# First edge stage of a graph-network kernel: both halves of a group's sums moved around the first filter layer, one group later

## The chip, the core and the metric

The kernel runs on one core of one Trainium2 chip. The metric is the device time in microseconds (us) of one execution. Three timed runs of the kernel before gave 2712.55 us as their median, with 2710.3 and 2718.26 us as the ends.

## What is computed

The reference is two layers of a graph network over 3125 nodes with 256 features and 50000 edges; each layer is a graph step and then a feed-forward step. The change touches only the first graph step, which is a continuous-filter convolution. Cut to what matters:

```python
W   = ssp(e_ji_basis @ fw1.T + fb1) @ fw2.T + fb2      # filter, one row per edge
W   = W * C[:, None]                                   # C from the edge's weight
h   = x @ w1.T                                         # node table
msg = h[src] * W                                       # gather, multiply
agg = jax.ops.segment_sum(msg, dst, num_segments=n)    # sum by target node
```

`ssp(x)` is `softplus(x) - log(2)`. The edges come sorted by target node.

## The kernel before, in words

The program is a row of stages with a barrier between them: preparation, the node table (`source_features`), the first edge stage (`edges_first`), the node update (`nodes_first`), a mixture of experts, the attention layer with an edge stage of its own (`attention_edges`), and the last feed-forward step. Each engine has its instructions written out by hand, in order, and engines meet only through semaphores. What matters here is `edges_first`.

The edges are cut into tiles of 256, and the 25 windows of 128 target nodes into the same list, so that there are 220 items of one tile and one window each. A **group** is two items, that is four chunks of 128 edges; there are 110 groups. For a group n the work is:

- SyncE loads the edge attributes `ea` (L533), four buffers, loaded seven groups ahead.
- ScalarE copies the group's source indices into `idx` (L319, `source_index`), and GpSimd gathers the node rows with four indirect transfers (L312, `gather`) into `rows`, four buffers of it, three groups ahead.
- TensorE computes the first filter layer into PSUM, two matmuls of 512 columns: `z(n)` (L581), two buffers.
- ScalarE takes Exp (L626) and Ln (L628) of it into `soft`, VectorE takes the result `hid` (L661), ScalarE rounds that to its high part `hidh` (L636), VectorE forms the low part `hidl` (L644). Each has two buffers.
- TensorE computes the second filter layer, 28 matmuls of 256 columns: `w(n)` (L592 to L596), in one PSUM buffer `wp`.
- VectorE builds the four scaled one-hot tiles `hot` (L652) and multiplies `wp` with the gathered rows into `msg` (L670), two buffers each.
- TensorE adds each item into the running window: `add(n, 0)` and `add(n, 1)`, two matmuls each (L567, `add_item`). There are two PSUM banks for windows, used in turn. After each item ScalarE copies the bank's sum to SBUF (L614) and clears the *other* bank (L615, `keep`), and the next item's matmuls wait for that (semaphore `s_acc`).

So between two items there is a round trip: TensorE ends an item, ScalarE copies and clears, TensorE may begin the next item. That holds for every pair of items, within a group and across groups.

The order on each engine is given by a function `step`, called once per group; `at(k)` is the group k ahead of the step's own n. Before the change TensorE's step n was

```python
add(n, 0);  z(n + 4);  w(n + 1);  add(n, 1)
```

and ScalarE's was

```python
keep(n, 0);  exp, ln(n + 4);  idx(n + 4);  hidh(n + 3);  keep(n, 1)
```

and VectorE's is `hot(n + 1)`, `hid(n + 3)`, `hidl(n + 2)`, `msg(n + 1)`. `rounds` (L293) writes the first steps out, puts the middle into a hardware loop of `UNROLL` steps a round, and writes the last steps out. `UNROLL` is 4. A buffer's number is the group's number modulo the number of buffers (`slot`, `slot4`), and `turn4` counts how often a buffer was used. The attention stage has a class of its own (`Edges`) and gathers of its own, so it does not use what is changed here.

Of the kernel before, what the change touches and what calls it, by code (L numbers as in the profile page):

```python
# [16 lines left out]
F32 = mybir.dt.float32  # L17
F32R = mybir.dt.float32r
I32 = mybir.dt.int32
# [234 lines left out]
class Group:  # L254


    COUNT, UNROLL = NIG, 4

    def __init__(self, it, q):
        self.n = it * 4 + q  # L260
        self.slot, self.turn = q % 2, it * 2 + q // 2
        self.slot4, self.turn4 = q % 4, it + q // 4
# [44 lines left out]
def gather(c, pool, g, idx, rows, table, s_rows, s_idx, s_used):  # L307


    need(pool, c.sem("poolgate"), (s_idx, g.n + 1), (s_used, g.n - 3))  # L310
    for j in range(IG):
        c.nc.gpsimd.indirect_dma_start(out=rows[:, g.slot4, j, :], out_offset=None, in_=table,  # L312
                                       in_offset=bass.IndirectOffsetOnAxis(ap=idx[:, g.slot4, j:j + 1], axis=0)).then_inc(s_rows[g.slot4], 16)


def source_index(c, act, g, idx, s_rows, s_idx):

    need(act, c.sem("actgate"), (s_rows[g.slot4], g.turn4 * 64))
    c.nc.scalar.copy(idx[:, g.slot4, :], c.src_i[:, bass.ds(g.n * IG, IG)]).then_inc(s_idx, 1)  # L319
# [169 lines left out]
def edges_first(c, A):  # L489
# [7 lines left out]
    with ExitStack() as s:  # L497
# [20 lines left out]
        s_rows = [c.sem(f"e1_rows{p}") for p in range(4)]  # L518
# [3 lines left out]
        with nc.Block() as block:  # L522
# [20 lines left out]
            @block.gpsimd  # L543
            def _(pool):
                nc.gpsimd.memset(zero[:, :], 0.0).then_inc(s_zero, 1)
                pool.wait_ge(s_zero, 1)
                nc.gpsimd.memset(ea[GA:P, :, :], 1.0 / GA).then_inc(s_cst, 1)
                pool.wait_ge(s_cst, 1)

                def step(at):  # L550
                    g = at(3)
                    if real(g):
                        gather(c, pool, g, idx, rows, c.h_dram, s_rows, s_idx, s_msg)
                rounds(pool, step, 3, 0)

            @block.tensor
            def _(pe):
# [4 lines left out]
                def add_item(g, j, wins):  # L562

                    need(pe, None, (s_msg, g.n + 1), (s_acc, g.n * JG + j), own=True)
                    for half in range(CT):
                        t = j * CT + half
                        last = mm(bank(wins[j]), hot[:, g.slot, t, :], msg[:, g.slot, t, :], start=False, stop=False, skip_group_check=True)  # L567
                    last.then_inc(s_agg, 1)

                def step(at):  # L570
                    a = at(0)
# [4 lines left out]
                    if real(g):  # L576
# [5 lines left out]
                        last.then_inc(s_z, 1)  # L582
                    g = at(1)
                    if real(g):

                        need(pe, None, (s_hl, g.n + 1), (s_msg, g.n), own=True)
                        for j in range(IG):
# [3 lines left out]
                            for k in range(KC):  # L591
                                mm(w, hidl[:, g.slot, cols[k]], w2h[:, k, :], start=(k == 0), stop=False)  # L592
                                mm(w, hidh[:, g.slot, cols[k]], w2l[:, k, :], start=False, stop=False)  # L593
                            mm(w, share[:, :], b2hl[:, :], start=False, stop=False)
                            for k in range(KC):
                                last = mm(w, hidh[:, g.slot, cols[k]], w2h[:, k, :], start=False, stop=(k == KC - 1))  # L596
# [44 lines left out]
            @block.vector  # L641
            def _(dve):
# [3 lines left out]
                def one_hot(g):  # L646
                    if real(g):

                        need(dve, s_dg, (s_agg, (g.n - 1) * JG))
                        for j in range(IG):  # L650
                            i = g.n * IG + j
                            v.scalar_tensor_tensor(hot[:, g.slot, j, :], c.iota_n[:, :], c.dst_rel[:, bass.ds(i, 1)],  # L652
                                                   c.coef[:, bass.ds(i, 1)].broadcast_to([P, P]), ALU.is_equal, ALU.mult)

                def step(at):
# [7 lines left out]
                    if real(h):  # L663

                        need(dve, s_dg, (s_hh, h.n + 1))
                        low(hidl[:, h.slot, :], hid[:, h.slot, :], hidh[:, h.slot, :]).then_inc(s_hl, 1)
                    if real(g):

                        need(dve, s_dg, (s_w, g.n + 1), (s_rows[g.slot4], (g.turn4 + 1) * 64))
                        v.tensor_tensor(msg[:, g.slot, :, :], wp[:, :].rearrange("p (a d) -> p a d", a=IG), rows[:, g.slot4, :, :], ALU.mult).then_inc(s_msg, 1)  # L670
# [1256 lines left out]
```

## Time and profile before

| | us |
|---|---|
| median of three timed runs | 2712.55 |
| lowest and highest of them | 2710.3, 2718.26 |
| the profiled execution's own time | 2724.59 |
| its span in the trace | 2722.8 |

| stage | from | to, in us of the span |
|---|---|---|
| first edge stage, its first steps | 81 | 124 |
| its even part | 124 | 1007 |
| its last steps, with no first layer left | 1007 | 1035 |

All times below are microseconds from the start of the span. The profiled execution took 12.0 us more than the median of the timed runs, and 1.8 us more than its span. A row of the timeline gives start, duration, engine, line, operation, what is written and what is read, and how many instructions were merged; in brackets the idle time of the engine before it and what ended it. An "x4" of a 32-bit matmul line is two matmuls, since the trace holds two records for each. The end of a matmul is modelled, so that records of matmuls that follow each other overlap.

### The profile page before, as it was taken

How to read it: one execution, taken by the hardware profiler on the slowest of the kernel's cores; microseconds unless marked ns; L12 is line 12 of the kernel's file. 1: busy time of each engine (PE TensorE's matmuls, PEld its weight loads, DVE VectorE, ACT ScalarE, POOL GpSimd, SP SyncE). 2: the span in 40 equal slices, each digit the busy share in tenths (PEclk: the TensorE clock that was granted, in tenths of full speed). 3: DMA queues.
4: the chain of work that ended last, by engine and by line, in shares of the span. 5: the costliest groups of instructions: out<-in, count | busy, mean ns of one | idle time of the engine just before them, and what ended most of it. 6: DMA issues, size and time to landing. Idle time of an engine off the chain costs nothing. (4 is left out here: it accounts for less than half of the span.)

```text
span 2722.8 us, 44123 instructions
## 1 busy us (share of the span) xinstructions
PE 2098.0 (77%) x11608; PEld 1731.4 (64%) x11609; DVE 1692.7 (62%) x3111; ACT 880.7 (32%) x1743; POOL 1098.4 (40%) x1037
## 2 busy tenths in 40 slices
PE   5588888888888888699995757877777777753498
PEld 4366666666666667699995645655555555532498
DVE  4355555555555554656556538887878788858565
ACT  2355555555555544344441101111111111100143
POOL 0355555555555544500001046555665656311200
PEclk8799999999999998799998968888989889867699
DMA  3222222222222220200000355554545545310100
GB/s 99 91 80 77 77 80 78 77 77 79 78 78 79 77 62 1 78 1 0 0 1 16 123 158 145 144 155 139 162 140 147 150 143 150 97 49 3 33 20 29
DMA packets 104782, 222.93 MB, mean 82 GB/s; under 512 B 19802, under 2 KB 58726, under 8 KB 104550
## 3 DMA queue, kind: packets, MB, share of 16 engines
q0 software_dynamic: 56320, 173.07, 21.9%
q1 hardware_dynamic: 48358, 48.68, 5.5%
q8 instruction: 40, 0.66, 0.1%
q14 instruction: 64, 0.52, 0.1%
HBM read 205.29 MB, written 16.38 MB: 81 GB/s over the span
## 5 line engine op out<-in xcount | busy, mean ns | idle before, releaser
L312 POOL DMA_INDIRECT e_rows<-h_table,e_idx x440 | 511.6, 1163 | 419.9 <-ACT e_idx L319 308.5
L1404 POOL DMA_INDIRECT a_rows<-kv_table,a_idx x440 | 466.2, 1060 | 389.6 <-issue 150.9
L670 DVE TENSOR_TENSOR e_msg<-e_w,e_rows 128x1024 f32<-128x1024 f32 x110 | 134.7, 1225 | 438.8 <-PE e_w L596 423.0
L1471 PE MATMUL a_q<-q,a_spread 128*128 x880 | 273.8, 465 | 126.4 <-ACT a_spread L1447 91.4
L567 PE MATMUL e_agg<-e_msg,e_hot 128*128 128x256 f32 x880 | 238.6, 394 | 169.8 <-ACT e_agg L615 153.0
L1471 PEld LDWEIGHTS a_q<-q,a_spread 128*128 128x128 f32 x880 | 191.2, 228 | 174.6 <-issue 145.6
L567 PEld LDWEIGHTS e_agg<-e_msg,e_hot 128*128 128x128 f32 x880 | 150.9, 190 | 225.3 <-issue 213.6
L592 PE MATMUL e_w<-w2h,e_hidl 128*128 128x256 f32 x880 | 271.2, 331 | 0.0
L1480 PE MATMUL a_agg<-a_rows,x 128*128 128x264 f32 x880 | 242.7, 424 | 18.7 <-DVE a_rows L1537 18.4
L1447 ACT COPY a_spread<-a_hotT 128x512 f32<-128x512 f32 x110 | 64.4, 585 | 522.7 <-PE a_hotT L1495 325.0
L593 PE MATMUL e_w<-w2l,e_hidh 128*128 128x256 f32 x880 | 227.8, 281 | 0.0
L1480 PEld LDWEIGHTS a_agg<-a_rows,x 128*128 128x128 f32 x880 | 188.1, 215 | 60.7 <-DVE a_rows L1537 16.3
L581 PE MATMUL e_z<-e_ea,w 128*128 128x512 f32 x440 | 210.3, 601 | 11.0 <-DMA e_ea<-in_eaT 8.7
L593 PEld LDWEIGHTS e_w<-w2l,e_hidh 128*128 128x128 f32 x880 | 166.7, 189 | 25.9 <-issue 25.9
L592 PEld LDWEIGHTS e_w<-w2h,e_hidl 128*128 128x128 f32 x880 | 166.1, 189 | 25.9 <-issue 25.6
L596 PE MATMUL e_w<-w2h,e_hidh 128*128 128x256 f32 x880 | 176.0, 281 | 0.0
L636 ACT CAST e_hidh<-e_hid 128x1024 fp32r<-128x1024 f32 x110 | 115.0, 1046 | 125.7 <-issue 74.5
L614 ACT COPY sums<-e_agg x220 | 81.9, 372 | 224.6 <-PE e_agg L567 212.7
L1550 DVE TENSOR_TENSOR a_rows<-a_q,a_rows 128x1024 f32<-128x1024 f32 x110 | 133.7, 1216 | 32.4 <-remote 18.6
L1531 DVE TENSOR_TENSOR sums<-sums,a_agg 128x264 f32 x220 | 93.5, 425 | 91.4 <-issue 47.4
L661 DVE SCALAR_TENSOR_TENSOR e_hid<-e_soft,e_z 128x1024 f32<-128x1024 f32 x110 | 133.4, 1213 | 20.8 <-ACT e_soft L628 20.8
L626 ACT ACTIVATE e_soft<-e_z 128x1024 f32<-128x1024 f32 x110 | 112.9, 1026 | 92.7 <-PE e_z L581 46.9
(338 smaller groups left out, 4705.3 us busy)
## 6 DMA issues: line engine op xcount, KB each, us to landing
e_ea<-in_eaT SPq DMA_DIRECT2D x220, 64.0 KB
e_rows<-h_table,e_idx POOLq DMA_INDIRECT x440
a_rows<-kv_table,a_idx POOLq DMA_INDIRECT x440
kv_table<-q_kv SPq DMA_DIRECT2D x25, 256.0 KB, 2.0
m_stage<-in_m_w SPq DMA_DIRECT2D x16, 256.0 KB, 2.7
x<-in_x SPq DMA_DIRECT2D x1, 3200.0 KB, 12.6
h_table<-n_h SPq DMA_DIRECT2D x5, 640.0 KB
x_table<-x SPq DMA_DIRECT2D x1, 3200.0 KB, 13.9
```

The costliest lines, as they stand in the source:

```text
L312: c.nc.gpsimd.indirect_dma_start(out=rows[:, g.slot4, j, :], out_offset=None, in_=table, in_offset=bass.IndirectOffsetOnAxis(ap=idx[:, g.s ...
L567: last = mm(bank(wins[j]), hot[:, g.slot, t, :], msg[:, g.slot, t, :], start=False, stop=False, skip_group_check=True)
L581: last = mm(z, w1[:, cols], ea[:, g.slot4, :], start=True, stop=True)
L592: mm(w, hidl[:, g.slot, cols[k]], w2h[:, k, :], start=(k == 0), stop=False)
L593: mm(w, hidh[:, g.slot, cols[k]], w2l[:, k, :], start=False, stop=False)
L596: last = mm(w, hidh[:, g.slot, cols[k]], w2h[:, k, :], start=False, stop=(k == KC - 1))
L661: v.scalar_tensor_tensor(hid[:, h.slot, :], soft[:, h.slot, :], SP_CAP, zp[h.slot][:, :], ALU.min, ALU.max).then_inc(s_hid, 1)
L670: v.tensor_tensor(msg[:, g.slot, :, :], wp[:, :].rearrange("p (a d) -> p a d", a=IG), rows[:, g.slot4, :, :], ALU.mult).then_inc(s_msg, 1)
L1404: nc.gpsimd.indirect_dma_start(out=rows[:, g.slot * IG + j, 0:2 * D], out_offset=None, in_=c.kv_dram, in_offset=bass.IndirectOffsetOnAxis( ...
L1471: last = mm(qp[g.pair][:, j * D:(j + 1) * D], spread[:, g.pair, j, :], window(c.q, wins[j // CT]), start=True, stop=True)
L1480: last = mm(ap[j][:, 0:DM], hot[:, t, :], rows[:, t, D:ROW], start=(half == 0), stop=(half == CT - 1))
L1550: v.tensor_tensor(keys, qp[i.pair][:, :].rearrange("p (a d) -> p a d", a=IG), keys, ALU.mult).then_inc(s_pr, 1)
```

## The change

In `edges_first`:

- TensorE's step n becomes `add(n - 1, 0)`, `z(n + 4)`, `add(n - 1, 1)`, `w(n + 1)`: the two sums of a group stand on both sides of the first layer, and one step later.
- ScalarE's step n becomes `keep(n - 1, 0)`, `hidh(n + 3)`, `keep(n - 1, 1)`, `exp, ln(n + 4)`, `idx(n + 7)`.
- VectorE's order stays. `hot`, `msg`, `hidh` and `hidl` have four buffers in place of two, and their waits are relaxed to match; `hidl` and `msg` each get a wait more, for the buffer that they now write.
- GpSimd's step gathers for `n + 6` in place of `n + 3`; `rows` and `idx` have eight buffers in place of four.
- `UNROLL` is 8, with `slot8` and `turn8`. The loops start up to seven groups early and run one step longer.

The arithmetic is the same, instruction for instruction.

The loop, the gather's wait and the buffers:

```diff
-    COUNT, UNROLL = NIG, 4
+    COUNT, UNROLL = NIG, 8
...
-    need(pool, c.sem("poolgate"), (s_idx, g.n + 1), (s_used, g.n - 3))
+    need(pool, c.sem("poolgate"), (s_idx, g.n + 1), (s_used, g.n - 7))
...
-        hidh = c.sb("e1_hidh", [P, 2, KC * W2], F32R, s)
-        hidl = c.sb("e1_hidl", [P, 2, KC * W2], F32R, s)
-        idx = c.sb("e1_idx", [P, 4, IG], I32, s)
-        rows = c.sb("e1_rows", [P, 4, IG, D], F32, s)
-        msg = c.sb("e1_msg", [P, 2, IG, D], F32, s)
-        hot = c.sb("e1_hot", [P, 2, IG, P], F32, s)
+        hidh = c.sb("e1_hidh", [P, 4, KC * W2], F32R, s)
+        hidl = c.sb("e1_hidl", [P, 4, KC * W2], F32R, s)
+        idx = c.sb("e1_idx", [P, 8, IG], I32, s)
+        rows = c.sb("e1_rows", [P, 8, IG, D], F32, s)
+        msg = c.sb("e1_msg", [P, 4, IG, D], F32, s)
+        hot = c.sb("e1_hot", [P, 4, IG, P], F32, s)
```

GpSimd's step:

```diff
-                    g = at(3)
+                    g = at(6)
```

TensorE's step:

```diff
-                    a = at(0)
+                    a = at(-1)
                     if real(a):
                         sums = item_windows(pe, c, a.n)
                         add_item(a, 0, sums)
...
                         last.then_inc(s_z, 1)
+                    if real(a):
+                        add_item(a, 1, sums)
                     g = at(1)
...
                         last.then_inc(s_w, 1)
-                    if real(a):
-                        add_item(a, 1, sums)
-                rounds(pe, step, 4, 0)
+                rounds(pe, step, 4, 1)
```

ScalarE's step:

```diff
-                    a = at(0)
+                    a = at(-1)
                     if real(a):
                         wins = item_windows(act, c, a.n)
                         keep(a, 0, wins)
+                    g = at(3)
+                    if real(g):
+
+                        need(act, s_ag, (s_hid, g.n + 1), (s_w, g.n - 3))
+                        nc.scalar.copy(hidh[:, g.slot4, :], hid[:, g.slot, :]).then_inc(s_hh, 1)
+                    if real(a):
+                        keep(a, 1, wins)
                     g = at(4)
...
-                    g = at(4)
+                    g = at(7)
                     if real(g):
                         source_index(c, act, g, idx, s_rows, s_idx)
-                    g = at(3)
-                    if real(g):
-
-                        need(act, s_ag, (s_hid, g.n + 1), (s_w, g.n - 1))
-                        nc.scalar.copy(hidh[:, g.slot, :], hid[:, g.slot, :]).then_inc(s_hh, 1)
-                    if real(a):
-                        keep(a, 1, wins)
-                rounds(act, step, 6, 0)
+                rounds(act, step, 7, 1)
```

VectorE's waits:

```diff
-                        need(dve, s_dg, (s_agg, (g.n - 1) * JG))
+                        need(dve, s_dg, (s_agg, (g.n - 3) * JG))
...
-                        need(dve, s_dg, (s_hh, h.n + 1))
+                        need(dve, s_dg, (s_hh, h.n + 1), (s_w, h.n - 3))
...
-                        need(dve, s_dg, (s_w, g.n + 1), (s_rows[g.slot4], (g.turn4 + 1) * 64))
+                        need(dve, s_dg, (s_w, g.n + 1), (s_agg, (g.n - 3) * JG), (s_rows[g.slot8], (g.turn8 + 1) * 64))
```

How the instructions stand is shown at two places. First TensorE, in the steps that are written out after the loop; line numbers of the changed kernel are one to three higher. `TENSOR_LOAD` reads the group's window numbers. Before:

```order
L596 MATMUL e_w<-w2h,e_hidh 128x256 x2
L567 ISA [waits e1_acc,e1_msg]
...
L567 MATMUL e_agg<-e_msg,e_hot 128x256 x2
L330 TENSOR_LOAD g_row
L330 ISA x2
L567 REGISTER_ALU [waits e1_acc,e1_msg]
...
L567 MATMUL e_agg<-e_msg,e_hot 128x256 x2
L581 MATMUL e_z<-e_ea,w 128x512 [waits e1_hid,e1_ea1]
L581 MATMUL e_z<-e_ea,w 128x512
L592 MATMUL e_w<-w2h,e_hidl 128x256 [waits e1_msg,e1_hidlow]
```

The same place in the changed kernel, here from the loop's body:

```order
L599 MATMUL e_w<-w2h,e_hidh 128x256 x2
...
L331 TENSOR_LOAD g_row
...
L568 REGISTER_ALU [waits e1_acc]
...
L568 MATMUL e_agg<-e_msg,e_hot 128x256 x2
...
L582 MATMUL e_z<-e_ea,w 128x512 [waits e1_hid]
L582 MATMUL e_z<-e_ea,w 128x512
L288 REGISTER_ALU [waits e1_msg]
L568 ISA [waits e1_acc]
...
L568 MATMUL e_agg<-e_msg,e_hot 128x256 x2
L595 MATMUL e_w<-w2h,e_hidl 128x256 [waits e1_msg,e1_hidlow]
```

The two items of a group had stood next to the neighbouring group's items, with only the load of the window numbers between; now the first layer (L582) stands between the two waits for `e1_acc` on one side, and the second layer (L595 to L599) on the other.

Second ScalarE, in the loop's body. Before:

```order
L330 TENSOR_LOAD g_row
...
L614 COPY sums<-e_agg 128x256
...
L615 COPY e_agg<-e_zero 128x256
...
L626 ACTIVATE e_soft<-e_z 128x1024 [waits e1_z]
L628 ACTIVATE e_soft<-e_soft 128x1024 [waits e1_exp]
L319 ISA [waits e1_rows1]
L319 COPY e_idx<-src_i 128x4
L287 REGISTER_ALU [waits e1_hid]
L636 CAST e_hidh<-e_hid 128x1024 [waits e1_w]
```

After it stands the second pair of L614 and L615. In the changed kernel:

```order
L331 TENSOR_LOAD g_row
...
L615 COPY sums<-e_agg 128x256
...
L616 COPY e_agg<-e_zero 128x256
L627 CAST e_hidh<-e_hid 128x1024 [waits e1_hid,e1_w]
...
L615 COPY sums<-e_agg 128x256
...
L616 COPY e_agg<-e_zero 128x256
L634 ACTIVATE e_soft<-e_z 128x1024 [waits e1_z]
L636 ACTIVATE e_soft<-e_soft 128x1024 [waits e1_exp]
...
L320 COPY e_idx<-src_i 128x4
```

The rounding of `hidh` (now L627) moved from behind Exp, Ln and the index copy to between the two keeps, and no longer waits for the second layer of the step before, but for one two groups older.

## Rows read from the trace of the kernel before

**Rows 1.** Busy time by stretch: length, PE, PEld, DVE, ACT, POOL busy (instructions), PEclk, DMA share, GB/s
```profile
200.00:600.00 400.00, 333.79 (x1897) 261.40 (x1896) 217.64 (x336) 215.23 (x382) 223.80 (x192) 1.00 0.26 78
```
**Rows 2.** Waits between 200 and 1000 us: total, times, longest
```profile
DVE e_msg L670 <- PE e_w L596: 371.1, 96, 3.9
...
ACT sums L614 <- PE e_agg L567: 174.9, 95, 1.9
...
PE e_agg L567 <- ACT e_agg L615: 131.2, 95, 1.5
```
**Rows 3.** Timeline, TensorE over one group from 501.8 us
```profile
501.82 1.02 PE L567 MATMUL e_agg<-e_msg,e_hot 128*128 128x256 f32 x4
...
504.25 1.12 PE L567 MATMUL e_agg<-e_msg,e_hot 128*128 128x256 f32 x4 [1.40 <-ACT e_agg L615]
...
505.21 1.88 PE L581 MATMUL e_z<-e_ea,w 128*128 128x512 f32 x4
...
507.05 0.28 PE L593 MATMUL e_w<-w2l,e_hidh 128*128 128x256 f32 x1
...
510.24 1.02 PE L567 MATMUL e_agg<-e_msg,e_hot 128*128 128x256 f32 x4
```
**Rows 4.** Timeline, ScalarE in the same group
```profile
505.75 0.37 ACT L614 COPY sums<-e_agg  x1 [1.86 <-PE e_agg L567]
506.06 0.38 ACT L615 COPY e_agg<-e_zero 128x256 f32 x1
...
507.21 1.03 ACT L626 ACTIVATE e_soft<-e_z 128x1024 f32<-128x1024 f32 x1 [0.78 <-issue]
...
508.36 1.06 ACT L628 ACTIVATE e_soft<-e_soft 128x1024 f32<-128x1024 f32 x1
...
509.32 0.18 ACT L319 COPY e_idx<-src_i 128x4 int32 x1
...
510.51 1.05 ACT L636 CAST e_hidh<-e_hid 128x1024 fp32r<-128x1024 f32 x1 [1.01 <-issue]
```
**Rows 5.** Timeline, VectorE in the same group
```profile
502.16 1.23 DVE L670 TENSOR_TENSOR e_msg<-e_w,e_rows 128x1024 f32<-128x1024 f32 x1 [3.79 <-PE e_w L596]
...
503.30 1.13 DVE L652 SCALAR_TENSOR_TENSOR e_hot<-iota_n,dst_rel,coef 128x128 f32<-128x128 f32 x4
...
504.35 1.21 DVE L661 SCALAR_TENSOR_TENSOR e_hid<-e_soft,e_z 128x1024 f32<-128x1024 f32 x1
...
505.48 1.22 DVE L644 TENSOR_TENSOR e_hidl<-e_hid,e_hidh 128x1024 fp32r<-128x1024 f32 x1
```
**Rows 6.** Timeline, GpSimd: third and fourth gather of a group
```profile
504.43 0.94 POOL L312 DMA_INDIRECT e_rows<-h_table,e_idx  x1 [0.30 <-issue]
...
505.68 1.84 POOL L312 DMA_INDIRECT e_rows<-h_table,e_idx  x1 [0.30 <-issue]
```
**Rows 7.** Timeline, the stage's first steps
```profile
90.02 1.15 POOL L312 DMA_INDIRECT e_rows<-h_table,e_idx  x1 [9.35 <-ACT e_idx L319]
...
97.61 0.40 PE L596 MATMUL e_w<-w2h,e_hidh 128*128 128x256 f32 x2
...
109.89 0.95 POOL L312 DMA_INDIRECT e_rows<-h_table,e_idx  x1 [0.30 <-issue]
...
113.10 1.04 ACT L636 CAST e_hidh<-e_hid 128x1024 fp32r<-128x1024 f32 x1 [15.04 <-issue]
...
123.99 1.22 DVE L670 TENSOR_TENSOR e_msg<-e_w,e_rows 128x1024 f32<-128x1024 f32 x1 [6.28 <-PE e_w L596]
```
**Rows 8.** Timeline, the stage's last steps
```profile
1006.84 1.23 DVE L670 TENSOR_TENSOR e_msg<-e_w,e_rows 128x1024 f32<-128x1024 f32 x1 [4.12 <-PE e_w L596]
...
1029.45 1.13 PE L567 MATMUL e_agg<-e_msg,e_hot 128*128 128x256 f32 x4 [1.48 <-ACT e_agg L615]
```
**Rows 9.** Busy time, a stretch of the experts stage, columns as in Rows 1
```profile
1170.00:1190.00 20.00, 20.00 (x158) 20.00 (x156) 9.90 (x18) 7.71 (x12) 0.00 (x0) 1.00 0.01 2
```
**Rows 10.** Timeline, ScalarE in the attention's edge stage, amid gathers
```profile
2002.55 0.59 ACT L1447 COPY a_spread<-a_hotT 128x512 f32<-128x512 f32 x1 [9.45 <-DMA e_rows<-h_table,e_idx]
```

More of the change, by code:

```diff
@@ L307, in gather @@
 def gather(c, pool, g, idx, rows, table, s_rows, s_idx, s_used):
-    need(pool, c.sem("poolgate"), (s_idx, g.n + 1), (s_used, g.n - 3))
+    need(pool, c.sem("poolgate"), (s_idx, g.n + 1), (s_used, g.n - 7))
     for j in range(IG):
-        c.nc.gpsimd.indirect_dma_start(out=rows[:, g.slot4, j, :], out_offset=None, in_=table,
-                                       in_offset=bass.IndirectOffsetOnAxis(ap=idx[:, g.slot4, j:j + 1], axis=0)).then_inc(s_rows[g.slot4], 16)
+        c.nc.gpsimd.indirect_dma_start(out=rows[:, g.slot8, j, :], out_offset=None, in_=table,
+                                       in_offset=bass.IndirectOffsetOnAxis(ap=idx[:, g.slot8, j:j + 1], axis=0)).then_inc(s_rows[g.slot8], 16)
 def source_index(c, act, g, idx, s_rows, s_idx):
-    need(act, c.sem("actgate"), (s_rows[g.slot4], g.turn4 * 64))
-    c.nc.scalar.copy(idx[:, g.slot4, :], c.src_i[:, bass.ds(g.n * IG, IG)]).then_inc(s_idx, 1)
+    need(act, c.sem("actgate"), (s_rows[g.slot8], g.turn8 * 64))
+    c.nc.scalar.copy(idx[:, g.slot8, :], c.src_i[:, bass.ds(g.n * IG, IG)]).then_inc(s_idx, 1)
 def item_values(eng, g, row, most):
@@ L517, in edges_first @@
         s_ea = [c.sem(f"e1_ea{p}") for p in range(4)]
-        s_rows = [c.sem(f"e1_rows{p}") for p in range(4)]
+        s_rows = [c.sem(f"e1_rows{p}") for p in range(8)]
         s_idx, s_ag, s_pg, s_dg = c.sem("e1_idx"), c.sem("e1_agate"), c.sem("e1_pgate"), c.sem("e1_dgate")
@@ L550, in step @@
                 def step(at):
[L551 removed]
+                    g = at(6)
                     if real(g):
                         gather(c, pool, g, idx, rows, c.h_dram, s_rows, s_idx, s_msg)
[L554 removed]
+                rounds(pool, step, 6, 0)
             @block.tensor
@@ L566, in add_item @@
                         t = j * CT + half
-                        last = mm(bank(wins[j]), hot[:, g.slot, t, :], msg[:, g.slot, t, :], start=False, stop=False, skip_group_check=True)
+                        last = mm(bank(wins[j]), hot[:, g.slot4, t, :], msg[:, g.slot4, t, :], start=False, stop=False, skip_group_check=True)
                     last.then_inc(s_agg, 1)
                 def step(at):
-                    a = at(0)
+                    a = at(-1)
                     if real(a):
@@ L591, in step @@
                             for k in range(KC):
-                                mm(w, hidl[:, g.slot, cols[k]], w2h[:, k, :], start=(k == 0), stop=False)
-                                mm(w, hidh[:, g.slot, cols[k]], w2l[:, k, :], start=False, stop=False)
+                                mm(w, hidl[:, g.slot4, cols[k]], w2h[:, k, :], start=(k == 0), stop=False)
+                                mm(w, hidh[:, g.slot4, cols[k]], w2l[:, k, :], start=False, stop=False)
                             mm(w, share[:, :], b2hl[:, :], start=False, stop=False)
                             for k in range(KC):
-                                last = mm(w, hidh[:, g.slot, cols[k]], w2h[:, k, :], start=False, stop=(k == KC - 1))
+                                last = mm(w, hidh[:, g.slot4, cols[k]], w2h[:, k, :], start=False, stop=(k == KC - 1))
                         last.then_inc(s_w, 1)
-                    if real(a):
-                        add_item(a, 1, sums)
-                rounds(pe, step, 4, 0)
+                rounds(pe, step, 4, 1)
             @block.scalar
@@ L663, in step @@
                     if real(h):
-                        need(dve, s_dg, (s_hh, h.n + 1))
-                        low(hidl[:, h.slot, :], hid[:, h.slot, :], hidh[:, h.slot, :]).then_inc(s_hl, 1)
+                        need(dve, s_dg, (s_hh, h.n + 1), (s_w, h.n - 3))
+                        low(hidl[:, h.slot4, :], hid[:, h.slot, :], hidh[:, h.slot4, :]).then_inc(s_hl, 1)
                     if real(g):
-                        need(dve, s_dg, (s_w, g.n + 1), (s_rows[g.slot4], (g.turn4 + 1) * 64))
-                        v.tensor_tensor(msg[:, g.slot, :, :], wp[:, :].rearrange("p (a d) -> p a d", a=IG), rows[:, g.slot4, :, :], ALU.mult).then_inc(s_msg, 1)
+                        need(dve, s_dg, (s_w, g.n + 1), (s_agg, (g.n - 3) * JG), (s_rows[g.slot8], (g.turn8 + 1) * 64))
+                        v.tensor_tensor(msg[:, g.slot4, :, :], wp[:, :].rearrange("p (a d) -> p a d", a=IG), rows[:, g.slot8, :, :], ALU.mult).then_inc(s_msg, 1)
                 rounds(dve, step, 6, 1)
```

9 lines of the change are left out of this document (5 added, 4 removed).

## The prediction, made before the changed kernel ran

> **What bounds the kernel now.** I read the profile in four steps. First the busy time by stretch. In the even part of the first edge stage TensorE is busy for 333.79 of 400 us at the full granted clock, every other engine for little more than half of the stretch [rows 1]. TensorE sets the pace there, but it idles for 66 us of the 400. Second, the waits say what it idles for: `add` (L567) waited 95 times for ScalarE's clearing of a bank (L615), 131.2 us in total between 200 and 1000 us, and no other wait of TensorE there comes near it [rows 2]. VectorE's longer wait, 371.1 us for the second layer, is that of an engine with time to spare. Third, the timeline of one group gives the shape of the wait: `add(n, 1)` of one group at 501.82, then 1.40 us idle, `add` of the next group at 504.25, first layer at 505.21, second layer, and `add(n, 1)` again at 510.24 [rows 3]. A group so takes 8.42 us. Over the whole even part it is the same: `msg` of group 1 starts at 123.99 [rows 7] and `msg` of group 106 at 1006.84 [rows 8], 882.85 us for 105 groups, **8.408 us a group**. This mean includes the hardware loop's jump at every fourth group, so the jumps cost nothing that is seen.
>
> Fourth, why only one of two round trips shows. A group has two: from `add(n, 0)` to `add(n, 1)`, behind 5 us of filter layers, and from `add(n, 1)` to the next group's `add`, with nothing between. The second is the 1.40 us.
>
> **The change, part by part.** The order on TensorE becomes `add(n-1, 0)`, `z(n+4)`, `add(n-1, 1)`, `w(n+1)`. No matmul is added or taken away. Both round trips now have a layer between.
>
> *TensorE's own need.* The idle time goes: 8.41 - 1.40 = 7.01 us. Two smaller things go with it. The end of `add` is modelled as 1.02 us after its start, while four records that follow on take 0.86 (the first layer starts 0.96 after an `add` that came out of a wait [rows 3], of which about 0.1 is that restart). So 0.17 of the 7.01 is drain that the next matmul would overlap, and 0.1 is the restart: 7.01 - 0.17 - 0.1 = 6.74. The same from the other side: from 505.21 to 510.24 the two layers take 5.03, two `add`s of 0.86 make it 6.75. TensorE's need is **6.75 us a group**; the upper end, if drain and restart stay, is 7.01.
>
> *Does the first layer cover its round trip?* `add` starts at 504.25, its modelled end is 505.37, ScalarE's copy starts at 505.75 and its clearing ends at 506.44 [rows 4]. So the 1.40 us of idle time are 0.38 to ScalarE, 0.69 on it and 0.33 back. `add(n-1, 1)` may thus start at 506.44 + 0.33 = 506.77. The first layer ends at 506.93: the second layer's matmuls stand 0.118 apart (27 of them from the second one at 507.05 to 510.24), so its first would stand there. It is covered, with 0.16 us to spare, if ScalarE is free when the first half is done. The other round trip has the second layer's 3.3 us over it.
>
> *Is ScalarE free?* Put the start of `add(n-1, 0)` at 0 and a group at 6.75. VectorE's `msg(n)` starts 0.34 after the second layer's end (501.82 and 502.16 [rows 3, 5]), `hot` 1.14 later, `hid(n+3)` 1.05 later [rows 5]: 0.34 + 1.14 + 1.05 = 2.53, and it ends at 3.74. `hidh` waits for it: with 0.12 from one instruction to the next through a semaphore, as from Exp's end to Ln, 3.86 to 4.91 [rows 4]. The second keep: 5.0 to 5.7 (0.69, as above). Its clearing is wanted at 6.75 - 0.33 = 6.4: covered by 0.7. Exp 1.03 and Ln 1.06 with 0.12 between, then the index copy, which starts before Ln's end: 5.7 + 1.03 + 0.12 + 1.06 + 0.08 = 8.0. The next group's first keep may start at 6.75 + 1.50 - 0.1 = 8.15. So ScalarE is free 0.15 us before it is needed: it fits, narrowly. The new place of `hidh` puts a wait for VectorE in front of the second keep, and behind it stand Exp, Ln and the index copy; it is the chain that is late next.
>
> *VectorE* needs 1.14 + 1.05 + 1.13 + 1.23 = 4.6 us of 6.75. *GpSimd* needs four gathers at 1.25, the fourth 0.9 longer (504.43 to 505.68 is 1.25; the fourth takes 1.84 [rows 6]): 5.9 us of 6.75. The new waits (`hidl` for a second layer of four groups before, `msg` for sums four groups before) are long met. The copies of the index and the gathers go three groups further ahead; past nothing that they would delay, since both engines have room. Cost: nothing in the even part.
>
> What the SBUF page bears on is that fourth gather. VectorE's `hidl` (L644), which has both inputs in SBUF, runs from 505.48 to 506.70, and the gather issued at 505.68 is the one that takes 1.84 us while `hidl` keeps its 1.22 [rows 5, 6]. The Trainium skill (SBUF — State Buffer, "Who interferes with whom") says that VectorE and GpSimd share a port pair as an exclusive lock, and that whichever issues second blocks fully. By that rule a new phase could also make `hidl` wait for a gather, up to 0.95 us; VectorE would need 5.6 of 6.75, and the sum would not move; the same rule is a rival below.
>
> I take 6.80 us a group, 6.75 with a little for margins this narrow. **Even part:** 105 x (8.408 - 6.80) = 169 us less.
>
> *Start.* GpSimd issues its first 16 gathers without a pause, 90.02 to 110.84. The second layer of group 0 ends at 98.0, but what waits for it on ScalarE starts only at 113.10, 2.3 us after the last of these gathers was issued [rows 7]. So the stage's first steps stand still for 15 us beside that row of gathers. Now eight buffers are filled, 32 gathers, of which 28 need no step with sums. They start earlier too: GpSimd had idled 9.35 us for the first index copy [rows 7], which stood behind the first Exp and Ln, and the first three now stand ahead of them, so the row may begin near 82. 28 to 32 gathers at 1.25 us end near 117 to 122. Bounds: 2 us less (an earlier start helps) and 20 us more (16 gathers more at 1.25, all of it waited for). I take **8 us more**, nearer to the middle, since part of the row is issued before the old one began.
>
> *End.* One step more: after the last second layer four `add`s follow one another in place of three, each a round trip of 1.12 + 1.48 [rows 8]: **2.6 us more**.
>
> Sum: -169 + 8 + 2.6 = **-158 us**. The profiled execution of 2724.6 becomes 2566, the median of 2712.5 (12 us less) becomes **2554**. The later stages are untouched. A full TensorE held its clock at 1.00 for 20 us in the experts stage [rows 9], so I charge nothing for a clock.
>
> **The rivals.**
>
> *ScalarE's chain is the new bound.* For: 0.15 us of room, and a late first keep moves `add(n-1, 1)`, so the second layer, so `msg`, `hid` and `hidh`. Against: the sum above fits. With a chain late by 0.2 to 0.8 us a group it is 7.0 to 7.6; at 7.3, 105 x 1.108 = 116, less 11: 105 us gained, **2607**. Decides from 0.15 us of extra delay. Chance 0.22.
>
> *The gathers are the new bound*: if in the new phase two or three gathers of a group are lengthened as the fourth is, each costs 0.9 more, and 5.9 becomes 6.8 or 7.7. At 7.7: 105 x 0.708 = 74, less 11: **2649**. Against: only `hidl` lengthened a gather in the group shown. Chance 0.03. The lock that the Trainium skill's page named above describes would be the mechanism.
>
> *The old round trip only moves*: ScalarE reaches the first keep so late that 1.40 us is idle in the middle of the step. Then only the cost at start and end is left, 11 us: **2723**, and the change does not do what it says. Against: the first layer's 1.72 us lies inside. Chance 0.03.
>
> *Slower: the standstill of the start comes into every group.* The same thing that held back TensorE's result from 98.0 to 113.10 is seen again amid the attention's gathers, where ScalarE idled 9.45 us before 2002.55 [rows 10]. Now GpSimd pauses for 2.8 us a group (8.4 less 5.6 from the first gather's start to the fourth's end); at 6.8 it would pause 1.2. If that is too short and each second group stands still for 4 us (a quarter of the 15), a group is 6.8 + 2 = 8.8: 105 x 0.39 = 41 us lost, plus 11: **2765**. It decides from a pause under about 1 us. Against: six gathers in a row went by at the start before anything was held. Chance 0.04.
>
> **How the numbers follow.** Forecast (6.75 to 7.0 a group) 0.68; the rivals 0.22, 0.03, 0.03, 0.04. The range reaches from the forecast's best (6.75, start 2 us cheaper: 174 less, about 2538, rounded down) to the ScalarE case at 7.45 a group: **2535 to 2622**. It leaves out the worst of that case and the last three. Measurement of this kernel tells about 0.3% from no change, 8 us: faster 0.94, same 0.02, slower 0.04.
>
> **What would show it.** Right: L568 in the changed profile waits for L616 next to never; TensorE over 90% busy in the even part; `msg` every 6.75 to 6.85 us; the first `msg` after 113. ScalarE's chain: L568 waits for L616 in the middle of each step, 0.2 us or more. The gathers: GpSimd without a pause, `msg` waiting for a transfer. The standstill: ScalarE or VectorE idle long after TensorE's records end. I am wrong if the time is over 2622 or if the gain lies in another stage.

## The result and the profile after

The changed kernel took 2617.32 us (median of four runs, 2606.0 to 2628.58) beside 2714.67 us for the kernel before: ratio 0.9643, 95% interval 0.9604 to 0.9683, so 97 us or 3.6% faster. The forecast was 2554 us, 158 us less, with a range of 2535 to 2622. The direction and the place of the gain were right, and the time lies inside the range, 5 us from its end; the size of the gain was not. One profiled execution, of 2628.58 us with a span of 2626.6, is read here.

First the busy time by stretch of the changed kernel, with the columns of [rows 1] and a second stretch behind it.

```profile
200.00:600.00 400.00, 373.35 (x2116) 296.49 (x2115) 240.88 (x371) 231.42 (x424) 226.51 (x212) 0.99 0.30 87
600.00:850.00 250.00, 241.88 (x1380) 192.24 (x1379) 155.64 (x240) 150.36 (x277) 144.99 (x139) 0.99 0.32 90
```

TensorE is busy for 373 of 400 us where it was for 334 [rows 1]. The waits of the changed kernel between 200 and 850 us (total, times, longest):

```profile
DVE e_msg L671 <- PE e_w L599: 128.0, 50, 5.7
ACT e_hidh L627 <- DVE e_hid L662: 116.3, 64, 2.7
POOL e_rows L313 <- ACT e_idx L320: 109.6, 41, 7.4
...
POOL e_rows L313 <- DVE e_msg L671: 69.7, 24, 5.2
...
ACT sums L615 <- remote: 45.8, 17, 5.7
...
PE e_agg L568 <- ACT e_agg L616: 17.2, 16, 2.3
...
PE e_agg L568 <- issue: 15.8, 25, 4.1
```

The wait that the change aims at, `add` for the cleared bank, fell from 107.6 us in 78 groups between the same 200 and 850 us (131.2 us in 95 groups up to 1000 us [rows 2]) to 17.2 us in 16. The change did its work; something else takes part of the gain. The `msg` rows say how much and where:

```profile
123.07 1.23 DVE L671 TENSOR_TENSOR e_msg<-e_w,e_rows 128x1024 f32<-128x1024 f32 x1 [22.07 <-remote]
...
130.77 1.23 DVE L671 TENSOR_TENSOR e_msg<-e_w,e_rows 128x1024 f32<-128x1024 f32 x1 [3.16 <-PE e_w L599]
...
903.95 1.23 DVE L671 TENSOR_TENSOR e_msg<-e_w,e_rows 128x1024 f32<-128x1024 f32 x1 [2.25 <-PE e_w L599]
```

From `msg(1)` to `msg(106)` it is 773.18 us for 105 groups, **7.364 us a group** where it was 8.408 and where 6.80 was forecast: 110 us gained of 169. The second `msg` starts 6.8 us later than in [rows 7]. What comes behind `msg(106)` is 6.7 us longer. The end of the stage is 3.9 of it: from `msg(106)` to the last `add`'s end it is 27.3 us before and 31.2 now. The other 2.8 is within what the later, untouched stages vary by (with them, all that comes behind `msg(106)` was 8 us shorter than before in a second profiled execution of the changed kernel). Sum: 110 less 6.8 less 6.7 is 96 us, the difference of the two profiled executions.

Now one group of the changed kernel. TensorE, GpSimd and VectorE, each from its own timeline:

```profile
644.42 1.05 PE L568 MATMUL e_agg<-e_msg,e_hot 128*128 128x256 f32 x4
```
```profile
640.64 1.06 POOL L313 DMA_INDIRECT e_rows<-h_table,e_idx  x1 [0.30 <-issue]
642.00 0.95 POOL L313 DMA_INDIRECT e_rows<-h_table,e_idx  x1 [0.30 <-issue]
643.25 0.97 POOL L313 DMA_INDIRECT e_rows<-h_table,e_idx  x1 [0.30 <-issue]
```
```profile
642.19 1.22 DVE L645 TENSOR_TENSOR e_hidl<-e_hid,e_hidh 128x1024 fp32r<-128x1024 f32 x1
645.40 1.23 DVE L671 TENSOR_TENSOR e_msg<-e_w,e_rows 128x1024 f32<-128x1024 f32 x1 [1.99 <-PE e_w L599]
```

The `add` at 644.42 directly follows the second layer, so the layer's last matmul is then issued and nearly done. VectorE has been free since 643.41, its message buffers are free and its rows are there, and yet `msg` starts at 645.40, 0.98 us after that `add`. Before it was 0.34 (501.82 and 502.16 [rows 3, 5]). Between 200 and 850 us this distance was 0.34 in the middle of 77 groups before and never over 0.5. Now its median is 0.97, it is over 0.5 in 56 of 88 groups, over 1.0 in 40 and over 1.8 in 8. The trace also records each semaphore event: that of the layer's last matmul, whose record ends at 644.58, stands at 645.23. So it is the event that is late, and not VectorE. In the kernel before, this event came 0.01 us behind the record's end in all 77 groups. In the group shown GpSimd has just issued a row of gathers when the layer ends: the last issue ends at 644.22. In the kernel before, the layer ended when GpSimd was just starting a new row.

Some holds are much longer. Here both the second layer and the `add` behind it are seen late, and the next `add` then waits for ScalarE's clearing:

```profile
439.66 1.02 PE L568 MATMUL e_agg<-e_msg,e_hot 128*128 128x256 f32 x4
...
441.87 0.95 POOL L313 DMA_INDIRECT e_rows<-h_table,e_idx  x1 [0.30 <-issue]
...
442.35 1.23 DVE L671 TENSOR_TENSOR e_msg<-e_w,e_rows 128x1024 f32<-128x1024 f32 x1 [5.65 <-remote]
...
443.32 0.37 ACT L615 COPY sums<-e_agg  x1 [3.57 <-remote]
...
444.33 1.13 PE L568 MATMUL e_agg<-e_msg,e_hot 128*128 128x256 f32 x4 [1.93 <-ACT e_agg L616]
```

From `msg(1)` to `msg(106)`, 13 of the 105 distances from one `msg` to the next are over 8 us. They hold 36 of the 59 us that the even part takes beyond 6.80 us a group.

### The profile page after: what moved, and what is told of

Read it like the earlier page. It is cut to its first block and busy times, and to the rows that moved or that the text cites. A ratio compares the mean times of both kernels' runs of the same rounds, so it can differ in the third digit from the quotient of the medians.

```text
span 2626.6 us, 43799 instructions
## 1 busy us (share of the span) xinstructions
PE 2102.3 (80%) x11608; PEld 1741.1 (66%) x11609; DVE 1694.7 (65%) x3111; ACT 864.0 (33%) x1743; POOL 1053.7 (40%) x1037
## 5 line engine op out<-in xcount | busy, mean ns | idle before, releaser
L313 POOL DMA_INDIRECT e_rows<-h_table,e_idx x440 | 467.8, 1063 | 341.1 <-ACT e_idx L320 135.5
L595 PE MATMUL e_w<-w2h,e_hidl 128*128 128x256 f32 x880 | 251.1, 307 | 17.9 <-DVE e_msg L671 17.9
L582 PE MATMUL e_z<-e_ea,w 128*128 128x512 f32 x440 | 212.8, 607 | 14.6 <-DMA e_ea<-in_eaT 14.6
L627 ACT CAST e_hidh<-e_hid 128x1024 fp32r<-128x1024 f32 x110 | 115.7, 1052 | 231.4 <-DVE e_hid L662 179.8
L595 PEld LDWEIGHTS e_w<-w2h,e_hidl 128*128 128x128 f32 x880 | 168.5, 191 | 22.2 <-issue 19.2
L599 PE MATMUL e_w<-w2h,e_hidh 128*128 128x256 f32 x880 | 177.3, 283 | 0.0
L1572 DVE TENSOR_REDUCE a_sc<-a_rows 128x32 f32<-128x1024 f32 x110 | 133.6, 1214 | 8.1
L582 PEld LDWEIGHTS e_z<-e_ea,w 128*128 128x128 f32 x440 | 85.4, 195 | 78.7 <-issue 64.3
```

What stands on the lines that cost most here:

```text
L313: c.nc.gpsimd.indirect_dma_start(out=rows[:, g.slot8, j, :], out_offset=None, in_=table, in_offset=bass.IndirectOffsetOnAxis(ap=idx[:, g.s ...
L582: last = mm(z, w1[:, cols], ea[:, g.slot4, :], start=True, stop=True)
L595: mm(w, hidl[:, g.slot4, cols[k]], w2h[:, k, :], start=(k == 0), stop=False)
L599: last = mm(w, hidh[:, g.slot4, cols[k]], w2h[:, k, :], start=False, stop=(k == KC - 1))
```

## The experiments

Two theories. **A: what TensorE has finished is seen late while gathers are under way**, and the change moved the gathers across the second layer's end. **B: ScalarE's chain** (`hid`, `hidh`, the second keep, Exp, Ln, index), the forecast's first rival, is simply too long. Ratios are to the kernel before, run on the same chip.

| run | us | ratio (95%) | us a group | first `msg` at |
|---|---|---|---|---|
| before | | 1 | 8.408 | 113.18 |
| changed | 2617.3 | 0.9643 (0.9604 to 0.9683) | 7.364 | 123.07 |
| e1_few_gathers | 2568.2 | 0.9417 (0.9382 to 0.9452) | 6.761 | 121.79 |
| e2_gather_after_w | 2567.5 | 0.9409 (0.9373 to 0.9445) | 6.874 | 105.90 |
| e3_before_deep_ring | 2743.6 | 1.0056 (1.0033 to 1.0078) | 8.403 | 122.67 |
| e4_old_ring | 2648.3 | 0.9698 (0.9659 to 0.9737) | 7.708 | 104.79 |
| e5_w_by_fp32 | 2651.6 | 0.9710 (0.9666 to 0.9755) | 7.468 | 124.12 |
| e6_before_late_gathers | 3245.5 | 1.1903 (1.1857 to 1.1949) | 13.304 | 108.36 |
| e7_quarter_rows | 2643.6 | 0.9688 (0.9649 to 0.9726) | 7.285 | 122.56 |
| e8_old_ring_after_w | 2621.7 | 0.9597 (0.9547 to 0.9647) | 7.342 | 105.91 |
| e11_changed_again | 2620.4 | 0.9672 (0.9633 to 0.9711) | 7.277 | 123.75 |
| e9_gather_before_w_end | 2541.4 | 0.9357 (0.9339 to 0.9375) | 6.781 | 103.89 |
| e10_index_earlier | 2541.9 | 0.9355 (0.9335 to 0.9375) | 6.803 | 101.94 |

**No gathers.** In `gather`:

```diff
+    if not (isinstance(g.n, int) and g.n < 8):
+        return
```

> The changed kernel whose first edge stage gathers source rows for its first eight groups only; all later groups multiply those old rows (the gathers of groups 8 to 107 are left out, with the waits for them). In the changed kernel a group took 7.36 us and msg started 0.98 us or more after the next add, where before it was 0.34. Theory A (TensorE's results are seen late while gathers are under way): with no gathers msg starts 0.34 us after the second layer's end again, a group takes 6.75 to 6.85 us, the gain over the changed kernel is 105 x 0.5 = 50 to 60 us, about 2560 us. Theory B (ScalarE's chain hid, hidh, second keep, Exp, Ln, index is too long by itself): a group stays at 7.2 to 7.4 us, 2605 to 2620 us.

Measured: 6.761 us a group. Timeline of one group, TensorE's row and VectorE's:

```profile
508.00 1.03 PE L570 MATMUL e_agg<-e_msg,e_hot 128*128 128x256 f32 x4
...
508.35 1.22 DVE L673 TENSOR_TENSOR e_msg<-e_w,e_rows 128x1024 f32<-128x1024 f32 x1 [2.21 <-PE e_w L601]
```

0.35 us, in all 96 groups between 200 and 850 us. By stretch:

```profile
200.00:600.00 400.00, 400.00 (x2371) 329.66 (x2371) 269.14 (x415) 256.99 (x473) 0.00 (x0) 1.00 0.07 19
```

TensorE has no idle time. ScalarE's order is untouched here, so theory B is out: the chain fits, as the forecast had worked out. A stands, though this run alone doesn't tell GpSimd's work from its transfers. (All groups from the ninth on multiply old rows, so the kernel computes something else.)

**Gathers tied to the second layer's end.** Group g's gathers also wait for the second layer of g-3:

```diff
-    need(pool, c.sem("poolgate"), (s_idx, g.n + 1), (s_used, g.n - 7))
+    need(pool, c.sem("poolgate"), (s_idx, g.n + 1), (s_used, g.n - 7), *more)
...
-                        gather(c, pool, g, idx, rows, c.h_dram, s_rows, s_idx, s_msg)
+                        gather(c, pool, g, idx, rows, c.h_dram, s_rows, s_idx, s_msg, (s_w, g.n - 2))
```

> The changed kernel in which the gathers of group g also wait for the second layer of group g-3, so that they begin when a second layer has just ended, and only three groups are gathered before the first second layer. Theory A: the gathers take 5.0 to 5.9 us of the 6.8 that pass until the next second layer ends, so few results meet a gather: a group takes 6.8 to 7.0 us, and the first msg starts near 103 instead of 123: about 2617 - 45 - 20 = 2550 us. If what counts is transfers still landing up to 1.6 us after the last issue, the results are late again and a group takes 7.3. Theory B: a group stays at 7.3 us and only the start is better: about 2597 us.

Measured: as many gathers as in the changed kernel, and one more wait, and in all it takes no longer than the run without gathers. That they are level is a coincidence of two parts: its even part is 12 us longer (6.874 against 6.761 us a group) and its first `msg` 16 us earlier. `msg` is still late, but evenly, by about 0.5 us (median distance 0.85, over 1.8 us once in 95 groups), and the chain has room for most of that. No distance from one `msg` to the next is over 8 us. So it is the long delays that hurt most in the changed kernel. Against that kernel the first `msg` is 17 us earlier.

**The deep ring alone**, on the kernel before: `rows` and `idx` with eight buffers, gathers six groups ahead, `UNROLL` 8, order of the sums as before.

> The kernel before with only the deeper ring of gathered rows (eight buffers, gathers six groups ahead, indices seven) and the loop of eight groups; the order of the sums as before. The start's price alone: first msg near 123 instead of 113.2, +10 us, about 2725 us (ratio 1.004) if the even part stays at 8.41 us a group. If the deeper ring (not the new order) is what makes TensorE's results late, msg starts up to 1 us after the second layer's end, and a group takes 8.6 to 9.2: 2745 to 2800 us.

Measured: the first `msg` 9.5 us later, 8.403 us a group. So the start's price is the ring's, and the ring holds nothing up in the even part. The whole kernel took 15.5 us more than the kernel before, where 10 was expected; the 6 us beyond the start are not explained by this stage's even part.

**The new order alone**, with the ring of before (four buffers, `at(3)`, `at(4)`, `s_used` at `g.n - 3`).

> The changed kernel with the ring of before (four buffers of rows and indices, gathers three groups ahead): the new order alone, msg and hot with four buffers. Start: first msg at 113 again, 10 us less. Even part: if the deeper ring makes the results late, 6.8 us a group and about 2550 us; if it is the new order (any gather under way when the second layer ends), 7.3 us a group and about 2607 us.

Measured: 7.708 us a group, worse than with the deep ring, so the new order by itself brings the delays. My expected start was wrong: the first `msg` came at 104.79 and not at 113, 3.2 us behind its layer, amid a row of gathers that went on without a pause (starts 1.25 us apart from 101.56 to 105.31); it was the second that was held, by 8.3 us, to 119.47. So a held result does not always wait for the row's end, and I can't say what let this one go. The long hold shown above from the changed kernel ended amid a row too.

**The semaphore on another matmul.** A small float32 matmul behind each second layer carries `s_w`:

```diff
+                        last = mm(wp[:, 0:8], c.ident[:, :], zero[:, 0:8], start=False, stop=True, skip_group_check=True)
                         last.then_inc(s_w, 1)
```

> The changed kernel with one small float32 matmul (8 columns of zeros added to the second layer's bank, 0.1 to 0.2 us) behind each second layer, which carries the semaphore in place of the layer's last float32r matmul. Theory A1 (only the completion of the float32r matmuls is held back while gathers are under way; the sums' and first layer's, in float32, were late only behind it): msg starts 0.3 us after this matmul in every group, a group takes 6.9 to 7.0 us, about 2575 us, and the start is not held (first msg near 106). Theory A2 (whatever TensorE completes there is held): msg is late as in the changed kernel, 7.4 to 7.5 us a group, 2620 to 2640 us, first msg at 123.

Measured: 7.468 us a group and the start held as before. A float32 matmul does not escape. The run is weaker than I meant it: this matmul stands right behind the layer, and if completions are held in order it is held behind it, whatever its type. The added matmul only adds zeros, and yet the sums of this run come out different, for which I have no reason. The changed kernel's own trace says more. The first layer, a float32 one, whose last record ends at 442.40 has its semaphore event at 446.49, although the event of the second layer before it came at 442.18. So results of float32 matmuls are held too, and not only behind a second layer.

**The test from the other side.** The kernel before, in which the gathers wait for the first layer of their step, so that they lie across the next second layer's end:

```diff
-                        gather(c, pool, g, idx, rows, c.h_dram, s_rows, s_idx, s_msg)
+                        gather(c, pool, g, idx, rows, c.h_dram, s_rows, s_idx, s_msg, (s_z, min(g.n + 2, NIG) if isinstance(g.n, int) else g.n + 2))
```

> The kernel before, its order, ring and loop unchanged, but its gathers also wait for the first layer of the same step, so that they run from 5.1 to some 11.7 us after the last second layer's end and are under way at the next one's (8.4 us). Theory A: msg starts 0.5 us or more late in most groups; in this order everything behind it is late by as much, so a group takes 8.8 to 9.6 us and the kernel 2760 to 2840 us, slower by 1.5 to 4.5%. If the deeper buffers or the new order are needed for the hold, it stays at 8.41 us a group, within 0.5%.

Measured: 3245 us, 19% slower; 13.3 us a group. Expected were 1.5 to 4.5%. One group, GpSimd and TensorE:

```profile
503.13 1.02 PE L567 MATMUL e_agg<-e_msg,e_hot 128*128 128x256 f32 x4
...
503.27 0.95 POOL L312 DMA_INDIRECT e_rows<-h_table,e_idx  x1 [0.30 <-issue]
...
504.52 0.95 POOL L312 DMA_INDIRECT e_rows<-h_table,e_idx  x1 [0.30 <-issue]
...
506.77 1.04 ACT L636 CAST e_hidh<-e_hid 128x1024 fp32r<-128x1024 f32 x1 [4.39 <-remote]
506.83 1.23 DVE L670 TENSOR_TENSOR e_msg<-e_w,e_rows 128x1024 f32<-128x1024 f32 x1 [8.65 <-remote]
...
508.70 2.07 PE L567 MATMUL e_agg<-e_msg,e_hot 128*128 128x256 f32 x4 [4.54 <-ACT e_agg L615]
```

The layer ends at about 503.1, two more gathers follow, the last ends at 505.47. VectorE *and* ScalarE, which wait for the same result, go on at 506.8, 3.7 us behind the layer's end where it was 0.34. In 90 of the 93 groups between 200 and 1450 us the layer's semaphore event came late, in the middle by 3.4 us, and 0.8 to 1.3 us behind the end of the last gather's issue. Nothing is changed but when the gathers are issued. In this order all the work behind `msg` is then late: TensorE idles for 4.54 us before the next `add`, and its granted clock falls. By stretch:

```profile
200.00:600.00 400.00, 269.59 (x1203) 194.58 (x1201) 136.51 (x210) 133.16 (x240) 114.03 (x122) 0.79 0.17 49
```

A mean of 0.79 (1.00 before) says that TensorE ran part of the time at the lower of its two levels: behind another such idle time, of 4.51 us, the first layer took 3.21 us from 496.77 us on, where it takes 1.88 at the full clock [rows 3]. That is the second part of the loss, which I had not expected; I did not separate the two. This is the strongest run for A.

**Fewer bytes.** From the ninth group on each gather fetches 256 bytes a row in place of 1024, with as many gathers.

> The changed kernel with as many gathers and descriptors, but from the ninth group on each fetches a quarter of a row (256 bytes in place of 1024; three quarters of each gathered row stay old). If it is the moved bytes that hold TensorE's completion back, the time in which they move is a quarter and most of the holds go: 6.8 to 7.0 us a group, 2565 to 2590 us. If it is the issue of the gathers and their descriptors, msg is late as in the changed kernel: 7.3 us a group, 2610 to 2625 us.

Measured: 7.285 us a group, within the spread of the changed kernel (7.364 and 7.277). The bytes are not what counts. What is left is the issue of the gathers, their descriptors, or the messages by which they report that they have landed; this run doesn't tell these apart. (Three quarters of each row stay old, so this kernel computes something else too.)

**Old ring, gathers after the second layer.**

> The new order with the ring of before (four buffers of rows, gathers three groups ahead), whose gathers wait for the second layer of three groups before: the run with the old ring (7.72 us a group) plus the wait that gave 6.88 us with the deep ring. Theory A (the phase of the gathers against the second layer's end decides, not how far ahead they run): 6.85 to 6.95 us a group, 2565 to 2575 us, ratio 0.941. If the deep ring is needed: 7.3 us a group or more, 2610 us.

Measured: 7.342, not 6.9. A miss that needed a reason. Its waits between 200 and 850 us:

```profile
DVE e_msg L671 <- PE e_w L599: 140.3, 54, 4.5
POOL e_rows L313 <- ACT e_idx L320: 118.0, 46, 5.7
```

GpSimd waits for the index copy, the last thing in ScalarE's step. With the ring of before the copy is made one step ahead of its gathers, so I took it that the copy, and not the added wait, sets their phase.

**The index copied one group earlier.** One number against that run:

```diff
-                    g = at(4)
+                    g = at(5)
                     if real(g):
                         source_index(c, act, g, idx, s_rows, s_idx)
```

> The run with the ring of before and gathers after the second layer (7.35 us a group) with ScalarE's copy of the indices five groups ahead in place of four: there GpSimd waited 46 times for that copy between 200 and 850 us, 118 us in total, so the copy and not the second layer set the gathers' phase. Theory A: with the copy done a group earlier the second layer sets the phase, 6.85 to 6.95 us a group as with the deep ring, about 2570 us, ratio 0.941; the eight buffers of rows are then not needed. If the deep ring itself is needed: 7.3 us a group, 2620 us.

Measured: 6.803 us a group, ratio 0.9355, better than expected. GpSimd still waited 46 times for the copy, but for 94.7 us and never over 2.2 us (118.0 and 5.7 before this edit), and 45 times for the second layer. So the phase decides and not the depth of the ring, and the eight buffers of rows are not needed.

**The gathers 0.83 us earlier still**, on the deep ring. The third of the second layer's four tiles raises a semaphore `s_w3`, for which the gathers wait in place of `s_w`:

```diff
+                            if j == IG - 2:
+                                last.then_inc(s_w3, 1)
```

> The changed kernel whose gathers wait for three quarters of a second layer (its third tile of four, 0.83 us before its end) in place of the whole one. In the run whose gathers wait for the end (6.88 us a group, 2567 us) msg still started 0.3 to 0.7 us late, since the fourth gather's transfer lands 0.6 us after the next second layer's end. Theory A: 0.8 us earlier the row of gathers is over when the layer ends, msg starts 0.18 us after its last matmul in most groups, a group takes 6.75 to 6.80 us, about 2557 us, ratio 0.937. If the hold only moves (the first gathers now lie across the end of the layer that releases them): msg late by 1 us or more, 6.9 to 7.4 us a group, 2570 us or more.

> The changed kernel itself, so that the next runs stand beside it on one chip: 2617 to 2635 us, ratio 0.964 to 0.966, 7.3 to 7.4 us a group.

Measured: 6.781 us a group, ratio 0.9357. The changed kernel, run again on the same chip, came to 0.9672 and 7.277 us a group, just outside the 7.3 to 7.4 and 0.964 to 0.966 expected of it. By the medians in the table the new version takes 79 us less than that, about 3%. `msg` starts over 0.5 us behind the layer in 10 of 95 groups. A group of it, GpSimd, TensorE and VectorE:

```profile
507.50 1.18 POOL L313 DMA_INDIRECT e_rows<-h_table,e_idx  x1 [0.30 <-issue]
...
509.74 1.02 PE L569 MATMUL e_agg<-e_msg,e_hot 128*128 128x256 f32 x4
...
510.09 1.22 DVE L674 TENSOR_TENSOR e_msg<-e_w,e_rows 128x1024 f32<-128x1024 f32 x1 [2.24 <-PE e_w L600]
...
510.55 0.94 POOL L313 DMA_INDIRECT e_rows<-h_table,e_idx  x1 [1.88 <-PE e_w L600]
```

The last gather's issue is over 1.06 us before the layer ends (508.68 against 509.74), and `msg` follows after 0.35 us, as before the change. This version and the one with the early index are both faster than either kernel; between the two there is no difference that was measured. They show that the forecast's 6.75 to 6.80 us a group is there to be had, with a wait *added*.

## Why the prediction was right and wrong, step by step

- **The range held the result, in part by luck.** Its upper end, 2622 us, came from the rival of ScalarE's chain at 7.45 us a group, and that chain was not the cause.
- **TensorE's own need, 6.75 us a group: right.** Without gathers 6.761 us, TensorE busy 400 of 400 us.
- **The first layer covers its round trip: right**, where the results are seen on time. Between 200 and 850 us `add` waits for the bank 16 times, not 78.
- **ScalarE's chain fits: right, and so the rival of 0.22 was given too much of a cause of its own.** Its room looks larger than the 0.15 us worked out: with `msg` late by 0.5 us in nearly every group, a group took only 0.11 us more than without gathers. Its time (2607) came nearest to the result, but by another mechanism: in the changed kernel it is not the chain's length but a late `msg`, with `hid` and `hidh` behind it, that makes the second keep late. A time near a rival's is no evidence for the rival; the run without gathers decided.
- **"Both engines have room" and "Cost: nothing in the even part", said of the index copies and gathers: the step that failed.** It was priced as engine time, and GpSimd had the time. What it left out is where in the group the gathers fall against the second layer's end. That was worth 7.364 - 6.80 = 0.56 us a group, 59 us, nearly the whole miss of 61. In [rows 3, 5, 6] both needed facts stood side by side: `msg` 0.34 us behind the layer, and the group's last gather over at 507.52, 2.7 us before the next layer ends.
- **The slower rival named the mechanism and had its size and its trigger wrong.** "The standstill of the start comes into every group" is what happened, though not as 4 us in each second group: between 200 and 850 us `msg` was late by 0.6 us in the middle and by 2.4 us at most, in 56 of 88 groups by more than 0.16. What decides is the phase and not a pause of GpSimd under 1 us. The run on the kernel before shows how large it can get: 3.4 us in nearly every group. I should have asked of this rival what it costs when it comes mildly.
- **Start, 8 us: right**, 9.9 us later for the first `msg`, 6.8 for the second; the ring alone gives 9.5.
- **End, 2.6 us: too small by about 1 us.** The stage's end took 3.9 us more, and 3.6 in the second profiled execution of the changed kernel. At the stage's very end TensorE has little work and its granted clock is 0.56 between 928 and 936 us (0.75 in the last 8 us before, 1028 to 1036), and the last two `add`s take 2.07 us each where the one at 926.90 took 1.12; the added step costs 2.07 + 1.48.
- **The fourth gather.** Gathers of 1.69 to 2.00 us still appear in the changed kernel, 38 of 440 beside 101 before, and the mean of the gathers between 200 and 850 us fell from 1166 to 1064 ns, so the rival of the gathers as bound did not come. In both kernels every one of them was issued while `hidl` ran, in the first half microsecond of it; a gather issued 1 us into `hidl` took 0.95 to 1.07 us. The Trainium skill (SBUF — State Buffer, "Who interferes with whom") says that whichever of the two issues second blocks, where VectorE's operation has two inputs in SBUF and GpSimd's instruction reads SBUF. For the gather issued second the trace fits that. The other way it doesn't: the `hidl` shown above starts at 642.19, inside the gather of 642.00 to 642.95, and takes 1.22 us; 63 of the 110 `hidl` began inside a gather's issue, and all took 1.210 to 1.224. Here the operation on VectorE was never blocked, and the measurement decides.

The same hold explains the start. The second layer of group 0 ends at 103.2 us in the changed kernel and its result is seen at 123.07; the last gather of the first row is issued from 118.37 on:

```profile
102.77 0.40 PE L599 MATMUL e_w<-w2h,e_hidh 128*128 128x256 f32 x2
...
118.37 0.94 POOL L313 DMA_INDIRECT e_rows<-h_table,e_idx  x1 [0.30 <-issue]
```

In the run whose gathers wait for the second layer, that layer ends at 105.72 with GpSimd idle since 98.61, and `msg` starts at 105.90.

## What to carry to other kernels

When a change moves the order of one engine, look at what it does to the phase of everything else in the loop, not only at busy time: a row of gathers that costs nothing where it stands can cost a good part of what the change gains (here 0.56 of 1.6 us a group), or more. If a result is seen late though its engine is done and its reader is free, see what GpSimd is issuing at that moment, and try moving the gathers with one more wait; here one added wait brought another 3%. And an odd stall at a stage's start is worth an experiment, since the same thing may come back in each turn of the loop.

## What the runs showed of the hardware

A finished result of TensorE can reach the waiting engines late while GpSimd issues a row of gathers: by 15 us at the start before the change, by 0.6 us in the middle and 2.4 us at most for the second layer in the changed loop between 200 and 850 us, by 3.4 us in nearly every group of the run with late gathers. There both waiting engines go on within 0.1 us of each other. They go on 1.2 to 1.4 us after the end of the last gather's issue in two of the groups shown, and 3.8 us after it at the changed kernel's start; but in the long hold shown, and with the new order on the old ring, a result was let go amid a row. A quarter of the bytes changed nothing.

Not every result is held. Before the change an `add` ended at about 505.4 between the third and fourth gather, and ScalarE started on it at 505.75 [rows 3, 4, 6]; the first layer ended at about 506.9 inside the fourth, and Exp started at 507.21 [rows 3, 4]. The semaphore events of all 156 sums there between 200 and 850 us came on time. What makes the difference stays open: it is not the kind of matmul alone, since a float32 first layer was held as well, and the length of the row so far was not tested by itself. By what path the semaphore is held stays open too.

A gather's issue is lengthened by a VectorE operation with both inputs in SBUF that already runs: from 0.95 us to 1.69 to 2.00 us when it is issued in the operation's first half microsecond. The VectorE operation itself kept its 1.22 us.

The attention stage may have the same hold: TensorE's record of `a_hotT` ended at about 1998.6 in the kernel before, amid gathers that went on, and ScalarE took it up at 2002.55 [rows 10]. Nothing was tried there.
